# The power layer moved into the block of the layers ahead of it, its first two batches prepared inside the last gated blocks

## The chip, the cores and the metric

One core of one Trainium2 chip runs the kernel. The metric is the device time of one execution in microseconds. Engines are named by their function: TensorE (PE in the rows), VectorE (DVE), ScalarE (ACT), GpSimd (POOL) and SyncE (SP), whose queue issues most DMAs.

## The reference

Two transformer layers on x of 16 batches x 256 tokens x 128. Each half adds the layer norm of its result to x.

```python
x = x + _layernorm(_L0_attn_ref(_layernorm(x), ...))   # softmax attention, 16 heads of 8
x = x + _layernorm(_L0_ffn_ref(_layernorm(x), ...))    # softmax attention, then 8 gated experts + a shared one
x = x + _layernorm(_L1_attn_ref(_layernorm(x), W))     # "power" attention
x = x + _layernorm(_L1_ffn_ref(_layernorm(x), ...))    # routed mixture with capacity

# the power attention
qkvgr = einsum('btc,oc->bto', x, W)                    # q, k, v, and one gate per head
log_g = log_sigmoid(gates); log_G = cumsum(log_g, axis=1)
S  = einsum('bhtd,bhsd->bhts', Q, K)
Z  = 2 * log(abs(S) + 1e-7) + log(scale) + log_G[t] - log_G[s], causal mask
P  = exp(Z - rowmax);  y = (P @ V) / sum(P)
```

The kernel computes P as (|S| + eps)^2 times exp of the decays log_G[t] - log_G[s].

## The kernel before, in words

The kernel is written out instruction by instruction, each engine with its own program, and engines meet at semaphores. It has these stages, one behind the other: `load_weights`, `soft_layers` (both softmax attentions as 32 steps) and `gated_layer` share one block; then come `power_layer`, `route` and `capped_mixture`, each with semaphores and a block of its own. Where such a stage ends (`semaphores`, L190) the semaphores are cleared and all engines meet at a barrier.

The gated layer (L1806) works on 8 blocks of 512 tokens. A block has 9 experts of 2 units, so 18 units q = 0 to 17, and there are 144 units n and 72 experts x in all. For a unit TensorE makes `gate_ps` and `up_ps` (3 products of 512 columns each, `hidden`, L1953), ScalarE the Silu (`gsg`), VectorE the product (`gprod`), ScalarE its high half and GpSimd its low half (`ghid`). Two experts later TensorE makes the down product (24 products of 128 columns, `down`, L1974), and VectorE adds it up (`gacc`). `gate_ps` has two banks, `up_ps` three. Block 7 is followed by a drain step: the last halves, the down products of experts 70 and 71, three sums, the layer norm and its addition to X.

The power layer (L817) works on 16 batches b with 8 units u each (n = 8 b + u). Step t runs the scores of batch t and, in the same step, parts of other batches at the places of `POWER_AT` (L813): T (transposes of the normalized rows), QK, V and CS (cumulated log gates) stand 14, 13, 10 and 7 units ahead of a batch's first score. They use one PSUM bank in turns. So the lead-in consists of the steps -3, -2 and -1, in which only batches 0, 1 and 2 are normalized, projected and spread. Behind QK, SyncE spreads the halves of Q and K over partitions with 12 DMAs a batch; behind CS, 6 DMAs write the decay rows into M. For unit n TensorE makes the decays (L1399, L1413), near blocks (L1417) and far scores (L1431), VectorE |score| (L1292), ScalarE exp of the decays (L1144) and the square (L1134), GpSimd their product (L955), and TensorE multiplies by V (L1447).

In the lead-in, `keep_awake` (L1385, products of L1388) gives TensorE work of no use between the waits; `AGAIN` (L1398) repeats the first decay product twice in each unit of batch 0 and of batches 14 and 15.

## Time and profile before

| What | us |
|---|---|
| median of 3 timed runs | 1249.94 (1248.51 to 1253.93) |
| the profiled execution, its own time | 1247.25 |
| its span, first to last instruction | 1245.5 |
| TensorE busy | 1130.0 (91%) |
| VectorE busy | 984.0 (79%) |
| ScalarE busy | 853.6 (69%) |
| GpSimd busy | 660.0 (53%) |
| mean granted TensorE clock | 0.96 |

Times of the trace are microseconds from the start of the span. The gated layer's last products end shortly before 788, the power layer's first instruction starts at 795.05, and its units run to about 1087. A busy share is a mean over stages with different limits, so a stage is read by windows and by its own timeline. The granted clock is a share of full speed: 1.00 is 2.4 GHz, 0.50 is 1.2 GHz, and a value between them is a mean over a window with both.

### The profile page before, as it was taken

What the parts mean: (1) busy time and instruction counts of PE and PEld (TensorE: products, weight loads), DVE (VectorE), ACT (ScalarE), POOL (GpSimd) and SP (SyncE); (2) the same over time, 40 slices, a digit from 0 to 9 for tenths busy, and PEclk for the clock granted to TensorE, in tenths of its full rate; (3) what the DMA queues carried; (4) which work ended last, traced back from release to release, by engine and by line L of the source; (5) the groups of instructions that cost most, each with busy time, mean ns of one, the idle gap of its engine ahead of it and who ended that gap; (6) DMA issues with size and microseconds to landing.
All of it is one profiled execution on the core that took longest, in us unless ns stands there. A gap on an engine that the chain in (4) does not pass through costs nothing. (4 is left out here: it accounts for less than half of the span.)

```text
span 1245.5 us, 33564 instructions
## 1 busy us (share of the span) xinstructions
PE 1130.0 (91%) x11805; PEld 636.4 (51%) x11805; DVE 984.0 (79%) x2700; ACT 853.6 (69%) x1834; POOL 660.0 (53%) x688
## 2 busy tenths in 40 slices
PE   5899999999999989999999999789999999947875
PEld 2344444444444444666666666436566665524652
DVE  4899999999999995788888888449799999864223
ACT  1688888888888887655565565258799999724314
POOL 3243343454334321566565566448688888725763
PEclk9999999999999998999999999889799999956998
DMA  4111111111111110000000000013122111023117
GB/s 118 34 39 40 41 41 36 40 39 43 40 39 41 41 28 2 1 2 2 2 1 2 2 2 1 5 33 99 44 55 56 39 35 38 19 81 93 49 47 202
DMA packets 83363, 48.91 MB, mean 39 GB/s; under 512 B 17335, under 2 KB 80256, under 8 KB 83200
## 3 DMA queue, kind: packets, MB, share of 16 engines
q1 hardware_dynamic: 80720, 42.62, 13.2%
q0 software_dynamic: 1792, 3.70, 1.1%
q8 instruction: 97, 1.59, 0.5%
q14 instruction: 66, 0.54, 0.1%
q10 hardware_dynamic: 688, 0.46, 0.1%
HBM read 16.52 MB, written 10.26 MB: 22 GB/s over the span
## 5 line engine op out<-in xcount | busy, mean ns | idle before, releaser
L626 DVE TENSOR_REDUCE mxsS<-scoreS 128x2 f32<-128x512 f32 x512 | 328.8, 685 | 40.9 <-PE scoreS L765 35.6
L514 ACT ACTIVATE PTS<-stS 128x512 f32<-128x512 f32 x512 | 283.5, 591 | 55.0 <-PE stS L769 54.6
L1912 POOL TENSOR_TENSOR ghid<-gprod,ghid 128x512 f16<-128x512 f32 x144 | 165.4, 1159 | 139.1 <-ACT ghid L2041 137.3
L765 PE MATMUL scoreS<-QK 31*128 31x256 f16 x1024 | 172.5, 280 | 25.8 <-DVE mxsS L626 13.8
L955 POOL TENSOR_TENSOR PTP<-PTP,EP 128x512 f32<-128x512 f32 x128 | 162.8, 1282 | 62.1 <-ACT PTP L1134 62.0
L769 PE MATMUL stS<-QK 32*128 32x256 f16 x1024 | 168.6, 277 | 1.3 <-ACT PTS L514 1.3
L690 PE MATMUL pvS<-PTS,Vx 128*32 128x256 f32 x2048 | 139.6, 391 | 0.4
L1292 DVE TENSOR_SCALAR AP<-score_psP 128x768 int32<-128x768 int32 x128 | 121.6, 950 | 23.1 <-PE score_psP L1431 22.3
L2041 ACT ACTIVATE ghid<-gprod 128x512 f16<-128x512 f32 x144 | 90.0, 625 | 65.9 <-DVE gprod L2144 65.8
L765 PEld LDWEIGHTS scoreS<-QK 31*128 31x128 f16 x1024 | 53.8, 93 | 147.2 <-DVE mxsS L626 94.5
L2035 ACT ACTIVATE gsg<-gate_ps 128x512 f32<-128x512 f32 x144 | 84.7, 588 | 54.4 <-PE gate_ps L1965 53.9
L1134 ACT ACTIVATE PTP<-AP,epsP 128x768 f32<-128x768 f32 x128 | 119.2, 931 | 3.1 <-DVE AP L1292 2.7
L387 POOL TENSOR_TENSOR rsS<-veS,halfS 128x2 f32<-128x2 f32 (+1 forms) x32 | 28.0, 874 | 172.4 <-DVE veS L594 90.4
L1970 PE MATMUL up_ps<-ghT,split 128*128 128x512 f16 x432 | 116.8, 379 | 0.0
L1965 PE MATMUL gate_ps<-ghT,split 128*128 128x512 f16 x432 | 116.7, 379 | 0.0
L2144 DVE TENSOR_TENSOR gprod<-gsg,up_ps 128x512 f32<-128x512 f32 x144 | 95.4, 682 | 26.6 <-ACT gsg L2035 18.7
L1982 PEld LDWEIGHTS down_ps<-split,ghid 128*128 128x128 f16 x1728 | 102.4, 98 | 17.1 <-POOL ghid L1912 0.6
L1982 PE MATMUL down_ps<-split,ghid 128*128 128x128 f16 x1728 | 108.1, 219 | 0.4 <-POOL ghid L1912 0.4
L1144 ACT ACTIVATE EP<-decay_psP 128x512 f32<-128x512 f32 x128 | 75.7, 591 | 29.6 <-PE decay_psP L1413 29.2
L690 PEld LDWEIGHTS pvS<-PTS,Vx 128*32 128x32 f32 x2048 | 54.1, 110 | 49.5 <-issue 21.6
L1970 PEld LDWEIGHTS up_ps<-ghT,split 128*128 128x128 f16 x432 | 42.1, 98 | 51.2 <-DVE gprod L2144 0.7
L2156 DVE SCALAR_TENSOR_TENSOR gacc<-down_ps,gcomb,gacc 128x128 f32<-128x128 f32 x224 | 62.7, 342 | 0.5 <-PE down_ps L1982 0.5
(321 smaller groups left out, 2246.9 us busy)
## 6 DMA issues: line engine op xcount, KB each, us to landing
QK<-HLS SPq DMA_DIRECT2D x384, 32.0 KB, 1.9
QK<-HLP SPq DMA_DIRECT2D x192, 32.0 KB, 1.9
expert_outputs<-tzero SPq DMA_DIRECT2D x8, 512.0 KB
cgot<-expert_outputs SPq DMA_DIRECT2D x16, 256.0 KB, 5.0
tokens<-XB SPq DMA_DIRECT2D x16, 128.0 KB, 2.4
out_dram<-X SPq DMA_DIRECT2D x8, 256.0 KB, 2.3
wi<-L_ffn_experts_inter_dram SPq DMA_DIRECT2D x1, 1792.0 KB, 9.2
wo<-n_L_ffn_experts_out_dram SPq DMA_DIRECT2D x7, 256.0 KB, 3.2
```

Of the source, the lines that this page charges most:

```text
L514: act.activation(PT[:, n % NPT, :], st_ps[:, (NS * t + n) % 3, :], ACT.Exp, scale=SCALE).then_inc(s_exp, 1)
L626: dve.tensor_reduce(mxs[:, u // 4, :, at], score_ps[:, n % 2, :].rearrange("p (c s) -> p c s", c=TC), AX.X, ALU.max).then_inc(s_max, 1)
L690: last = pe.matmul(pv_ps[32 * j:32 * j + 32, q], Vx[:, t % 3, c, 4 * g + j, :], PT[:, (4 * g + (j ^ 2)) % NPT, S * c:S * c + S], start=(c ...
L765: scored = pe.matmul(score_ps[:, k, cols], QK[part, new, g, 0, rows], QK[part, new, g, 1, :], start=True, stop=True)
L769: turned = pe.matmul(st_ps[:, (NS * t + n) % 3, cols], QK[part, old, g, 1, rows], QK[part, old, g, 0, :], start=True, stop=True)
L955: eng.tensor_tensor(w, w, E[:, n % NE, :], ALU.mult).then_inc(s_wd if n % NU in MULT_BY_DVE else s_wp, 1)
L1134: act.activation(PT[:, n % NW, :], A[:, n % NA, :], ACT.Square, bias=eps[:, 0:1]).then_inc(s_sq, 1)
L1292: dve.tensor_scalar(A[:, n % NA, :].bitcast(I32), score_ps[:, n % 2 * WU:n % 2 * WU + WU].bitcast(I32), 0x7FFFFFFF, None, ALU.bitwise_and) ...
L1912: pool.tensor_tensor(hid[:, n // FC % NHID, 1, c, :], prod[:, n % NPROD, :], hid[:, n // FC % NHID, 0, c, :], ALU.subtract).then_inc(s_hid, 1)
L1965: last = pe.matmul(gate_ps[:, n % 2, :], gate_w[:, lw, e, cols], hT[:, n // NQ % 2, lh, :], start=(k == 0), stop=(k == 2))
L1970: last = pe.matmul(up_ps[:, n % 3, :], up_w[:, lw, e, cols], hT[:, n // NQ % 2, lh, :], start=(k == 0), stop=(k == 2))
L1982: last = pe.matmul(down_ps[:, x % 2, t * D:(t + 1) * D], hid[:, x % NHID, lh, c, t * P:(t + 1) * P], down_w[:, lw, x % EX, c, :], start=(c ...
```

## The change

`power_layer` no longer opens a block. It takes its semaphores from the common set and returns one program for each engine and four guest functions, which other stages call at named places. Tiles come from regions with fixed offsets: its buffers lie where the experts' weights and the soft layers' tiles lay; PT over the gated layer's tiles; wi and wo over the gated weights. Those writers wait for the gated layer's last readers (`gated.s_hid`, `gated.s_down`, `gated.s_acc`, `gated.s_sg`, `gated.s_prod`).

- T, QK, V and CS of batches 0 and 1 run as guests in gated blocks 6 and 7, with the moments of batches 0 to 2, the fixed rows of M and the zeros of Vk. All of them use one PSUM bank. The steps of the power layer begin at 0.
- The root of the guests' layer norm is GpSimd's `pow` instead of ScalarE's Ln and Exp. The log sigmoid of the gates of both batches is made in one go (Abs, Exp, Ln). Their `fac` is copied out raw, and its Exp comes in the power layer's first step.
- `keep_awake` is gone, and so is `AGAIN` for batch 0.
- The gated drain step is cut up: down product 70 behind the near blocks of power unit 0, down product 71 in unit 1, the sums in units 0 and 1, the moments in unit 4, the root behind unit 6, the last addition in unit 1 of step 1.
- The moments of gated block 0 stand a few units earlier in the soft layers. Regions of later stages are laid out by hand; their instructions are the same.

The diff, cut to its core:

```diff
-    STEPS = range(-3, NB + 5)
-    AWAKE, AGAIN = {("T", 0): 24, ("QK", 0): 3, ("V", 0): 5, ("CS", 0): 4, ("QK", 1): 3, ("V", 1): 5, "scores": 6}, 2
+    STEPS, AGAIN, EARLY_CS = range(NB + 5), 2, 2
+    UNITS, ADDED = 144, 72
...
+        def guest_scalar(act, what, t):
...
+            elif what == "softplus":
+                act.wait_ge(free["V"], EARLY_CS)
+                act.activation(gl[:], gx[:], ACT.Abs).then_inc(s_ge, 1)
+                act.wait_ge(s_ge, 2 * EARLY_CS + 1)
+                act.activation(gl[:], gl[:], ACT.Exp, scale=-1.0).then_inc(s_ge, 1)
+                act.wait_ge(s_ge, 2 * EARLY_CS + 2)
+                act.activation(gl[:], gl[:], ACT.Ln, bias=1.0).then_inc(s_ge, 2 * EARLY_CS - 2)
...
+                if n == 0:
+                    act.wait_ge(gated.s_hid, UNITS)
+                if n == 2:
+                    act.wait_ge(gated.s_acc, ADDED)
                 act.activation(PT[:, n % NW, :], A[:, n % NA, :], ACT.Square, bias=eps[:, 0:1]).then_inc(s_sq, 1)
...
+            elif what == "gates":
+                dve.wait_ge(s_ge, 4 * EARLY_CS)
+                reach(dve, full["CS"], t)
+                dve.scalar_tensor_tensor(lg[:], gx[:, t, :, :], 0.0, gl[:, t, :, :], ALU.min, ALU.subtract)\
+                   .then_inc(s_lg, 1)
...
+        def cumulate(pe, t):
+            pe.wait_ge(s_lg if t < EARLY_CS else free["V"], t + 1)
...
             def decays(n):
                 t, u = n // NU, n % NU
-                if n == 0:
-                    keep_awake(AWAKE["scores"])
+                if n < 2:
+                    pe.wait_ge(gated.s_sg, UNITS - 1 + n)
                 if u == 0:
                     pe.wait_ge(s_m, 96 * (t + 1))
                 reach(pe, s_taken, n - 1)
-                for _ in range(AGAIN if t >= NB - 2 or t == 0 else 0):
+                for _ in range(AGAIN if t >= NB - 2 else 0):
...
+                gated.scalar(act, {(6, 15): guest("T", 0), (6, 17): guest("QK", 0), (7, 2): guest("V", 0),
+                                   (7, 3): guest("T", 1), (7, 5): guest("QK", 1), (7, 7): guest("V", 1),
+                                   (7, 8): guest("softplus", 0), (7, 11): guest("CS", 0), (7, 14): guest("CS", 1)})
+                power.scalar(act, {(0, 0): opening})
...
+                gated.drain_vector(dve, 0)
+                power.vector(dve, {(0, 0): lambda: gated.drain_vector(dve, 1), (0, 1): lambda: gated.drain_vector(dve, 2),
+                                   (0, 4): lambda: gated.drain_vector(dve, 3), (1, 1): lambda: gated.drain_vector(dve, 4)})
...
+                gated.tensor(pe, {(6, 14): guest("T", 0), (6, 16): guest("QK", 0), (7, 1): guest("V", 0),
+                                  (7, 3): guest("T", 1), (7, 4): guest("QK", 1), (7, 6): guest("V", 1),
+                                  (7, 10): guest("CS", 0), (7, 12): guest("CS", 1)})
+                power.tensor(pe, {(-1, 7): lambda: gated.drain_tensor(pe, 0), (0, 1): lambda: gated.drain_tensor(pe, 1)})
```

TensorE before, from the last gated unit over the barrier into the lead-in. L1965 and L1970 are the gate and up products, L1982 the down products of experts 69, 70 and 71, L1388 the filler:

```order
L1965 MATMUL gate_ps<-ghT,split 128x512 x3
L1970 MATMUL up_ps<-ghT,split 128x512 x3
L1982 MATMUL down_ps<-split,ghid 128x128 x72
L2483 UNCONDITIONAL_BRANCH
L1332 UNCONDITIONAL_BRANCH
L1388 MATMUL decay_psP<-cstb 128x512 x24
L1339 MATMUL miscP<-cst,yP 128x128 x2
L1388 MATMUL decay_psP<-cstb 128x512 x3
L1345 MATMUL miscP<-yTP,wq 128x256
L1345 MATMUL miscP<-yTP,wk 128x256
L1388 MATMUL decay_psP<-cstb 128x512 x5
L1350 MATMUL miscP<-wv,yTP 128x144 x2
```

TensorE after, from the last gated unit (L2088, L2093; down products L2067) into power unit 0 (L1491 to L1525). The rows of near blocks (L1507, L1511) alternate four times; two of the four stand here:

```order
L2088 MATMUL gate_ps<-ghT,split 128x512 x3
L2093 MATMUL up_ps<-ghT,split 128x512 x3
L2067 MATMUL down_ps<-split,ghid 128x128 x24
L1491 MATMUL decay_psP<-cstb 128x512
L1507 MATMUL decay_psP<-MP 128x128
L1511 MATMUL score_psP<-QK 128x128
L1507 MATMUL decay_psP<-MP 128x128
L1511 MATMUL score_psP<-QK 128x128
```

```order
L2067 MATMUL down_ps<-split,ghid 128x128 x24
L1525 MATMUL score_psP<-QK 128x128 x2
L1491 MATMUL decay_psP<-cstb 128x512
```

Between the last gated unit and the first decay product one down product is left of three, and neither a branch nor filler; the second piece follows the first one's near blocks.

TensorE after, units 136 to 138 of block 7. L1434 to L1438 are CS of batch 0, which before stood in the lead-in:

```order
L2088 MATMUL gate_ps<-ghT,split 128x512 x3
L2093 MATMUL up_ps<-ghT,split 128x512 x3
L1434 MATMUL misc_aP<-cst,lgP 16x256
L1435 MATMUL misc_aP<-cst,lgP 16x128
L1437 MATMUL misc_aP<-lgP,cst 128x16
L1438 MATMUL misc_aP<-lgP,cst 128x16
L2088 MATMUL gate_ps<-ghT,split 128x512 x3
L2093 MATMUL up_ps<-ghT,split 128x512 x3
L2067 MATMUL down_ps<-split,ghid 128x128 x24
L2088 MATMUL gate_ps<-ghT,split 128x512 x3
L2093 MATMUL up_ps<-ghT,split 128x512 x3
```

The four products of CS stand between unit 136 and unit 137, in the midst of gated work.

ScalarE before, at the seam. L2041 is the high half of units 142 and 143:

```order
L2041 ACTIVATE ghid<-gprod 128x512 x2
L2483 UNCONDITIONAL_BRANCH
L1053 UNCONDITIONAL_BRANCH
L1136 ACT_TABLE_LOAD
L1087 ACTIVATE lvP<-mvP,epsP 128x2
L1089 ACTIVATE rsP<-lvP 128x2
```

ScalarE after, units 133 to 136 of block 7. L2154 is Silu, L2141 the high half, L1112 to L1116 are Abs, Exp and Ln of the gates:

```order
L1107 ACTIVATE Vx<-misc_aP 128x32x8
L1109 ACTIVATE gxP<-misc_aP 128x32
L2154 ACTIVATE gsg<-gate_ps 128x512
L2141 ACTIVATE ghid<-gprod 128x512
L1112 ACTIVATE glP<-gxP 128x64
L1114 ACT_TABLE_LOAD
L1114 ACTIVATE glP<-glP 128x64
L1116 ACT_TABLE_LOAD
L1116 ACTIVATE glP<-glP 128x64
L2154 ACT_TABLE_LOAD
L2154 ACTIVATE gsg<-gate_ps 128x512
L2141 ACTIVATE ghid<-gprod 128x512
```

Three table loads stand between the Silu of unit 134 and that of unit 135, where before there was none between two Silus. The load at the power layer's start stays.

## Rows read from the trace of the kernel before

**Rows 1.** Windows of whole stretches; columns: window, us, busy (x count) of five engines, clock, DMA.

```profile
680.00:720.00 40.00, 38.53 (x369) 24.93 (x368) 35.48 (x116) 23.50 (x46) 24.65 (x23) 1.00 0.01 1
786.00:795.00 9.00, 1.51 (x24) 1.34 (x24) 5.14 (x22) 0.00 (x0) 1.20 (x2) 0.89 0.00 1
795.00:820.00 25.00, 18.80 (x79) 8.92 (x79) 5.16 (x20) 6.71 (x21) 9.85 (x11) 0.90 0.08 19
875.00:890.00 15.00, 15.00 (x127) 8.76 (x130) 9.44 (x23) 10.71 (x26) 10.54 (x11) 0.50 0.13 34
```

**Rows 2.** Timeline, block 7: start us, us, engine, line, operation [idle <- releaser].

```profile
776.50 0.81 PE L1965 MATMUL gate_ps<-ghT,split 128*128 128x512 f16 x3
...
777.35 0.60 ACT L2035 ACTIVATE gsg<-gate_ps 128x512 f32<-128x512 f32 x1 [1.21 <-PE gate_ps L1965]
...
777.84 0.62 ACT L2041 ACTIVATE ghid<-gprod 128x512 f16<-128x512 f32 x1
...
778.40 0.69 DVE L2144 TENSOR_TENSOR gprod<-gsg,up_ps 128x512 f32<-128x512 f32 x1 [1.66 <-ACT gsg L2035]
...
779.09 1.50 PE L1982 MATMUL down_ps<-split,ghid 128*128 128x128 f16 x24
...
780.43 0.81 PE L1965 MATMUL gate_ps<-ghT,split 128*128 128x512 f16 x3
```

**Rows 3.** Timeline, table load of the gated layer's start, softplus and log gates.

```profile
489.71 1.28 ACT L2035 ACT_TABLE_LOAD   x1
491.00 1.14 ACT L2035 ACTIVATE gsg<-gate_ps 128x512 f32<-128x512 f32 x2
...
807.66 0.23 ACT L1078 ACTIVATE geP<-geP 128x32 f32<-128x32 f32 x1
...
807.92 0.19 DVE L1193 SCALAR_TENSOR_TENSOR lgP<-miscP,geP 128x32 f32<-128x32 f32 x1 [1.88 <-ACT geP L1078]
```

**Rows 4.** Timeline, gated tail, SyncE's decay rows, TensorE's first decay, first score.

```profile
783.02 2.84 PE L1982 MATMUL down_ps<-split,ghid 128*128 128x128 f16 x48
...
815.34 3.44 SPq L979 DMA_DIRECT2D MP<-partsP  x6
...
820.00 0.67 PE L1398 MATMUL decay_psP<-cstb 128*128 128x512 bf16 x2 [4.27 <-DMA MP<-partsP]
...
821.88 0.96 DVE L1292 TENSOR_SCALAR AP<-score_psP 128x768 int32<-128x768 int32 x1 [6.20 <-PE score_psP L1431]
```

**Rows 5.** Windows, batches 0, 1, 3, 4 and 5 of the power layer.

```profile
821.88:839.26 17.38, 16.77 (x145) 7.68 (x144) 10.48 (x20) 13.27 (x27) 10.02 (x9) 0.85 0.11 27
839.26:854.75 15.49, 15.12 (x215) 9.31 (x214) 13.16 (x26) 13.62 (x27) 12.14 (x11) 1.00 0.50 153
...
870.16:893.28 23.12, 22.43 (x215) 12.91 (x214) 16.14 (x38) 15.56 (x33) 15.28 (x15) 0.63 0.16 40
893.28:909.37 16.09, 15.99 (x221) 9.95 (x220) 15.36 (x39) 14.42 (x33) 12.16 (x12) 1.00 0.15 41
909.37:925.44 16.07, 15.97 (x221) 9.96 (x220) 15.19 (x39) 14.96 (x35) 13.96 (x14) 1.00 0.21 57
```

**Rows 6.** Timeline, TensorE's V, decay, CS, T, QK and far score.

```profile
836.02 0.76 PE L1350 MATMUL miscP<-wv,yTP 128*128 128x144 f32 x4
...
840.70 0.39 PE L1399 MATMUL decay_psP<-cstb 128*128 128x512 bf16 x1
...
841.35 0.61 PE L1356 MATMUL miscP<-cst,lgP 128*16 128x256 f32 x2
...
842.65 0.28 PE L1431 MATMUL score_psP<-QK 31*128 31x128 f16 x2
...
843.52 0.44 PE L1339 MATMUL miscP<-cst,yP 128*128 128x128 f32 x2
...
845.54 0.70 PE L1345 MATMUL miscP<-yTP,wq 128*128 128x256 f32 x2
...
846.60 0.28 PE L1431 MATMUL score_psP<-QK 31*128 31x128 f16 x2
```

More of the change, by code:

```diff
@@ L986, in store @@
                 sp.dma_start(rows[:, part, 0:D], Y[:, part, :]).then_inc(s_stored, 16)
-            sp.wait_ge(s_zero, 5)
+            sp.wait_ge(s_zero, 9)
+            for t in range(2):
+                spread(t)
+            for t in range(EARLY_CS):
+                spread_decays(t)
             for t in STEPS:
                 if t == 1:
+                    sp.wait_ge(gated.s_down, ADDED)
                     sp.dma_start(wi[:], dram["L1_ffn_experts_inter"].rearrange("e d f -> d e f")).then_inc(s_w, 16)
@@ L996, in _ @@
                     store(t - 4)
-                if has(t + 1):
+                if t >= EARLY_CS - 1 and has(t + 1):
                     spread_decays(t + 1)
@@ new lines, in power_layer, with transposes, project @@
+        ident = cst[:, C_IDENT:C_IDENT + P]
+        def transposes(pe, t):
+            pe.wait_ge(s_y, 2 * t + 2)
+            for c in range(TC):
+                last = pe.transpose(bank("T")[:, c * P:(c + 1) * P], y[:, c, :], ident)
+            last.then_inc(full["T"], 1)
+        def project(pe, t):
+            pe.wait_ge(free["T"], t + 1)
+            for k, name in enumerate(("wq", "wk")):
+                last = pe.matmul(bank("QK")[:, k * S:(k + 1) * S], w[name][:], yT[:], start=True, stop=True)
+            last.then_inc(full["QK"], 1)
@@ L1438, in times_v @@
                 reach(pe, s_os, NG * t + g)
+                if t == 0 and g == 0:
+                    pe.wait_ge(gated.s_acc, ADDED)
                 if g == 0:
@@ L1449, in times_v @@
                 last.then_inc(s_pv, 1)
+            decays(0)
+            near_blocks(0)
+            guests[-1, 7]()
             for t in STEPS:
@@ L1950, in head_tensor, with down, drain_tensor, tensor @@
                 score(pe, 0)
-        def tensor(pe):
+        def down(pe, x):
+            pe.wait_ge(s_hid, FC * (x + 1))
+            if x < 2:
+                pe.wait_ge(soft.free[("PR", "YT")[x]], SOFT_STEPS)
+            reach(pe, s_acc, x - 1)
+            for t in range(TB):
+                for c in range(FC):
+                    for k, (lh, lw) in enumerate(PARTS):
+                        last = pe.matmul(down_ps[:, x % 2, t * D:(t + 1) * D],
+                                         hid[:, x % NHID, lh, c, t * P:(t + 1) * P], down_w[:, lw, x % EX, c, :],
+                                         start=(c == 0 and k == 0), stop=(c == FC - 1 and k == 2))
+            last.then_inc(s_down, 1)
+        def drain_tensor(pe, k):
+            down(pe, EXPERTS - 2 + k)
+        def tensor(pe, guests):
             def hidden(n):
@@ new lines, in rows_and_gates @@
+                def rows_and_gates():
+                    power.guest_vector(dve, "rows", 0)
+                    power.guest_vector(dve, "gates", 1)
+                soft.vector(dve, {(-3, 5): lambda: load.vector(dve), (last - 2, 6): lambda: gated.head_vector(dve, 0),
+                                  (last - 1, 1): lambda: gated.head_vector(dve, 1),
+                                  (last, 2): lambda: gated.head_vector(dve, 2),
+                                  (last, 5): lambda: gated.head_vector(dve, 3)})
```

557 lines of the change are left out of this document (322 added, 235 removed).

## The prediction, made before the changed kernel was run

> **What bounds the kernel now.** I first read the windows: the last steady stretch of the gated layer, the seam behind it, and the lead-in of the power layer [rows 1]. In the gated layer TensorE is busy for 38.53 of 40 us at full clock, VectorE for 35.48, ScalarE for 23.50 and GpSimd for 24.65: TensorE sets the pace. From 786 to 795 TensorE works for 1.51 of 9 us, and from 795 to 820 it shows 18.80 of 25 us, nearly all of it filler that keeps its clock up. In the same 25 us the useful engines work for 5.16 (VectorE), 6.71 (ScalarE) and 9.85 us (GpSimd): nothing is full, so this stretch is a chain of waits. Then I read the power layer batch by batch [rows 5]: from batch 4 on a batch takes 16.07 to 16.09 us with TensorE busy for 15.97 to 15.99, so TensorE is the bound there too, with VectorE (15.19) and ScalarE (14.96) close behind. Batch 0 (17.38) and batch 3 (23.12) are the odd ones, and both carry a lower granted clock. Last I read the timeline for the edges: the last gate and up products (unit 143) are over at 783.02, where the down products start; and the first |score| of the power layer (L1292, my mark for "batch 0 begins") starts at 821.88 [rows 4]. That is 38.9 us from 783.02, and the change attacks them.
>
> **What goes.** The gated drain, the barrier, and the lead-in (normalize, T, QK, V, CS of batch 0 and 1, their spreads over the DMA queue) all lie one behind the other in those 38.9 us. After the change the first score needs, behind 783.02: the down product of expert 69 (half of the 2.84 us of two, 1.42), decay and near blocks of unit 0 (840.70 to 841.35, 0.65), the down product of expert 70 (1.42), the far score (0.28). That is 3.8 us, so batch 0 would begin at 786.8 if nothing had been added earlier [rows 4, 6].
>
> **What is added on TensorE.** The lead-in products of two batches now stand in TensorE's row in the gated layer, where it is the bound, so they count in full: T 0.44, QK 1.06 (845.54 to 846.60), V 0.76, CS 1.30 (841.35 to 842.65), together 3.56 us, twice, 7.1 us [rows 6]. The filler and the doubled decay products of batch 0 go and cost nothing.
>
> **What is added elsewhere.** VectorE gets about the 5.16 us of the lead-in, GpSimd its 9.85 us and three roots that ScalarE took before, spread over the last two blocks, which last some 75 us (18 pairs of units at 3.93 and what is between them). VectorE has 4.5 us of slack in 40, GpSimd 15, and VectorE has no next block's moments and routing to do in block 7 [rows 1, 2]. I price both at nothing: TensorE's rings of two gate banks and three up banks cover a partner that is late by a unit, and it idles for only 1.5 us in 40 although VectorE is busy for 35.48. If that cover is gone, the bound is the whole 5.2 us.
>
> **What is added on ScalarE, the one wait I expect.** The gated layer uses Silu, the softplus of the gates Exp and Ln. The order shows three table loads around it (before Exp, before Ln, before the next Silu). A load takes 1.28 us and the next activation starts 0.01 us behind it [rows 3]. I count from the start of the gate product of unit 134, 0. Silu starts at 0.85 (776.50 to 777.35) and takes 0.60; the high part 0.62; Abs, Exp and Ln at 0.23 each 0.69, three loads 3.84: ScalarE is back at 6.60. Silu of unit 135 takes it to 7.20, VectorE's product (0.69) to 7.89, its log gates (0.19) to 8.08. TensorE meanwhile does a pair of units with its down product in 3.93 us (776.50 to 780.43) and a unit without one in 1.30 (half of 776.50 to 779.09), so unit 136 is over at 5.23; the next in its row is CS of batch 0, which waits for these log gates. It waits 2.9 us [rows 2, 3]. While it waits, all behind it waits, the gate product of unit 137 too; that one would have waited for ScalarE until 7.20 anyway, and is no second price. For CS of batch 1 ScalarE and VectorE are ready within some 0.1 us of TensorE by the same count. Bounds: 0 (the loads hide in ScalarE's idle time, 16.5 us in 40) and 8.1.
>
> The Trainium skill, "ScalarE: Activation LUTs", section "What ACT_TABLE_LOAD costs", puts every switch at about 2.66 us, a 1283 ns load and a drain of about 1380 ns. By that rule the three switches would take 4.1 us more, the wait would be 7.0 and not 2.9 us, and the end 4 us later than my sum. The trace agrees on the load and shows no drain behind it, at 489.71 after a running ScalarE.
>
> **The DMA queue.** Decay of unit 0 waits for the rows of M that SyncE issues in 3.44 us; TensorE went on at 820.00, 1.2 us behind the last issue of 815.34 [rows 4]. In the new order rows of batch 0 are ready at some 13.3 on the count above; 3.44 and 1.2 behind is 18. TensorE comes there at 783.02 + 1.42 less 764.7 (unit 134's start, four pairs of 3.93 before 780.43), 19.7, plus 2.9 and 2.6 for the two CS: 25. So it hides; a slip of 7 us would show. The wait for the down product of expert 71 ahead of the load of wi is over a batch earlier than SyncE comes to it.
>
> **Batch 0.** It begins at 786.8 + 7.1 + 2.9 = 796.8, 25.1 us earlier than 821.88. Its length: before, 17.38 at clock 0.85 with doubled decay products. Now TensorE has 11.1 us of work there (8 units of 0.65 + 0.28, one each of T, QK and V, one down product), ScalarE the 13.27 us of before and 0.6 for the last high part. Queued behind the waits: TensorE's down product 71 (1.42) waits for ScalarE's high part and GpSimd's low part of unit 143; VectorE's sum of it stands in front of |score| of unit 2; ScalarE's square of unit 2 waits for that sum. Behind the first far score TensorE has 0.65 + 0.28 + 0.65 + 1.42 = 3.0 us up to the end of down product 71; the sum is four VectorE instructions, 0.9 us at the tail's mean of 0.23 (22 in 5.14 us, rows 1). So unit 2 comes 3.9 us behind unit 0, where two units of a steady batch take 4.0. I take 15.5, as batch 1 has (15.49); bounds 13.9 (ScalarE's work alone) and 23.1 (a whole batch at the lower clock) [rows 5]. Gain 1.9 us.
>
> **The sum.** 25.1 + 1.9 = 27.0 us off the profiled execution's own 1247.25 (span 1245.5 and 1.75 around it): 1220.3. That execution is 2.7 us below the median of the timed runs (1249.94) and 1.3 below the fastest. Taken off the median it is 1222.9. I say 1222. The gated drain now lies beside batch 0 and 1, everything from batch 4 on is as it was.
>
> **The rivals.**
> A. As above, with one stretch at the lower clock as before: 1222, own range 1218 to 1227.
> B. The fall in batch 3 goes. There the granted clock is 0.50 (1.2 of 2.4 GHz) from 875 to 890 although TensorE shows 15.00 of 15 us busy, and the batch takes 23.12, not 16.09: 7.0 us. In the whole batch TensorE waited for only 0.7 us (22.43 busy) [rows 1, 5]. Batches 4 to 13 do the same work at 1.00. If the new start shifts this away: 1215. For it: it happens once in 14 like batches. Against it: it may belong to the order of work in batch 3, which is unchanged.
> C. The clock falls in batch 0. Without the doubled decays TensorE is busy for 11 of 15.5 us there, less than in any full batch of before, and no filler stands ahead. In batch 0 ScalarE hides the slower products, but the level held for some 17 us in batch 3, so half a batch or a whole one behind it pays up to 7.6 us (23.12 less 15.49): 1226 to 1230. The Trainium skill, "TensorE: Matmul & The Clock Gate", section "What's actually happening", says the default state is throttled and activity releases it. By that rule the seam's fall goes with the idle stretch, which is in A already; whether batch 0 has activity enough no row here shows.
> D. The table loads cost what the bound says (8.1 us and not 2.9), or VectorE's added work does: 1227.
> E. Slower than before. The clock falls at batch 0 and does not come back while batches are TensorE bound. Each batch at half costs 7.0 us, so the gain of 27.0 is gone after four batches, and from the fifth on it is over 0.5% slower: five batches give 1222 + 35 = 1257. For it: it held through a full TensorE once. Against it: it came back by itself after 17 us, and after the far longer idle of the seam within batch 0.
> That the change doesn't do what it says (batch 0 still waits for the gated end) would show as units 0 to 2 stretched by the last high and low part; by the order it is at most 3 us.
>
> **Chances.** A 0.54, B 0.16, C 0.18, D 0.08, E 0.04. From 1212 to 1232 holds all of A, nearly all of B, C and D. A measurement of this kernel tells a change from none from about 0.5% (6.2 us) on; all but E and accidents of the same size lie beyond it: faster 0.94, same 0.02, slower 0.04.
>
> **What would show it.** In the profile after: no gap over 2 us on TensorE between the last gated unit and the first score, and no filler; the |score| of unit 0 at about 797, that of batch 1 at 812; a wait of about 3 us on TensorE for VectorE's log gates in the middle of block 7, with three table loads on ScalarE ahead of it; no wait of the first decay product for a DMA; units 0 to 2 of batch 0 within 4 to 5 us; batches 1 and 2 at 15.5. The prediction is wrong if the gated blocks 6 and 7 grow by more than 12 us, if the first decay waits for M, or if the granted clock is at the lower level for more than one batch.

## The result, and the profile after

The changed kernel takes 1233.84 us (median of 18 runs, 1229.66 to 1246.35) against 1249.8 for the kernel before, run beside it (18 runs); ratio 0.9872, 95% interval 0.9849 to 0.9895. It is faster by 16 us. Forecast were 1222 and the range 1212 to 1232: the direction came out, the size did not, and of the 28 us that were to go 16 went. The profiled execution took 1234.57 us (span 1232.7), where the sum had given 1220.3: 14.3 us more.

First the windows of batch 0 to 3 in the profile after (us, then the busy time of each engine, the granted clock, the share of the DMA engines), each batch from its first |score| to the next one's:

```profile
800.63:818.64 18.01, 15.59 (x147) 8.42 (x146) 13.05 (x35) 12.59 (x23) 12.12 (x11) 0.72 0.05 14
818.64:840.37 21.73, 19.44 (x215) 11.63 (x214) 16.43 (x31) 13.93 (x28) 11.78 (x10) 0.76 0.35 110
840.37:855.78 15.41, 15.23 (x215) 9.30 (x214) 14.28 (x33) 13.96 (x29) 12.59 (x12) 1.00 0.13 35
855.78:872.37 16.59, 15.35 (x215) 9.30 (x214) 15.87 (x39) 14.13 (x32) 13.50 (x14) 1.00 0.17 47
```

Against [rows 5]: batch 0 and 1 are longer (17.38 and 15.49 before) and carry the lower clock. Batch 3 takes 16.59 and not 23.12, its clock is 1.00. Batch 0 begins at 800.63 where 796.8 was forecast.

The same view of two blocks of the gated layer, each from its first gate product to the next block's: block 5, which has no guests, and block 6, which has them.

```profile
671.59:709.38 37.79, 36.32 (x343) 23.18 (x341) 33.27 (x108) 22.20 (x44) 22.60 (x20) 1.00 0.01 1
709.38:752.02 42.64, 39.19 (x349) 25.37 (x347) 38.43 (x119) 22.79 (x46) 31.33 (x34) 0.96 0.01 2
```

Block 6 of the kernel before took 37.45 us, so the block is 5.2 us longer. T and QK of batch 0 explain 1.1 us of it: from the first start of each to the start of the product behind it are 0.22 and 0.86 us. Against block 5 VectorE is busy for 5.2 us more and GpSimd for 8.7. The timeline of that block, TensorE first, says where TensorE stops (the bracket is the idle time before, and what ended it; down products in between are left out):

```profile
733.40 0.81 PE L2088 MATMUL gate_ps<-ghT,split 128*128 128x512 f16 x3
736.19 0.82 PE L2093 MATMUL up_ps<-ghT,split 128*128 128x512 f16 x3 [1.98 <-DVE gprod L2298]
738.49 0.46 PE L2047 MATMUL gturn_ps<-router,ghT 128*128 128x8 f16 x12 [1.47 <-DVE ghT L2192]
...
740.72 2.53 PE L2067 MATMUL down_ps<-split,ghid 128*128 128x128 f16 x24
```

VectorE in the same place. `gve` is the variance, the input of the norm's root:

```profile
727.64 0.98 DVE L2274 TENSOR_SCALAR gve<-gmv 128x4 f32<-128x4 f32 x1
...
732.14 2.67 DVE L2280 TENSOR_SCALAR gtmp<-gacc,gmv,grs 128x128 f32<-128x128 f32 x4 [1.30 <-POOL grs L2006]
734.85 0.69 DVE L2283 TENSOR_TENSOR X<-X,gtmp 128x512 f32<-128x512 f32 x1
735.46 1.28 DVE L2298 TENSOR_TENSOR gprod<-gsg,up_ps 128x512 f32<-128x512 f32 x2
```

And GpSimd ahead of it. `yP` is a guest, `ghid` the gated layer's own low part, `grs` the root:

```profile
726.66 0.80 POOL L1040 TENSOR_SCALAR yP<-X,mvP,rsP 128x128 f32<-128x128 f32 x1
727.43 1.16 POOL L2011 TENSOR_TENSOR ghid<-gprod,ghid 128x512 f16<-128x512 f32 x1
728.58 0.79 POOL L1040 TENSOR_SCALAR yP<-X,mvP,rsP 128x128 f32<-128x128 f32 x1
729.95 1.16 POOL L2011 TENSOR_TENSOR ghid<-gprod,ghid 128x512 f16<-128x512 f32 x1 [0.58 <-ACT ghid L2141]
731.07 1.04 POOL L2006 TENSOR_TENSOR grs<-gve,ghalf 128x4 f32<-128x4 f32 x1
732.07 1.17 POOL L2011 TENSOR_TENSOR ghid<-gprod,ghid 128x512 f16<-128x512 f32 x1
733.17 1.05 POOL L1030 CAST MP<-cst 128x1024 bf16<-128x1024 f32 x1
```

The block's own norm on VectorE waits for a root that GpSimd gives at 732.1, 22.7 us behind the start of the block, where block 5 has it at 21.3. The way to that delay goes over VectorE. The guest at 726.66 pushes the low part to 727.43; the variance starts 0.21 us behind it and ends with it, after 0.98 us in place of the 0.17 of block 5. The product, ScalarE's high part, the next low part and the root behind it are late in turn. Ahead of that low part GpSimd is idle for 0.58 us, so the guest at 728.58 costs the root nothing. Then the four subtractions take 2.67 us beside GpSimd's low part and cast, where in block 5 they took 1.94; the product is late, and TensorE waits 1.98 us for it, a wait that block 5 does not have. The 1.47 us of wait a little later stand in block 5 too and are no child of the change. After that the down product of two halves takes 2.53 us and not 1.50: the clock has gone to its lower level.

In the middle of block 7 stands the wait that was forecast. ScalarE:

```profile
772.59 1.28 ACT L1114 ACT_TABLE_LOAD   x1
773.89 0.26 ACT L1114 ACTIVATE glP<-glP 128x64 f32<-128x64 f32 x1
774.22 1.28 ACT L1116 ACT_TABLE_LOAD   x1
775.51 0.26 ACT L1116 ACTIVATE glP<-glP 128x64 f32<-128x64 f32 x1
775.79 1.28 ACT L2154 ACT_TABLE_LOAD   x1
777.08 0.60 ACT L2154 ACTIVATE gsg<-gate_ps 128x512 f32<-128x512 f32 x1
```

VectorE, GpSimd and TensorE behind it:

```profile
777.71 0.69 DVE L2298 TENSOR_TENSOR gprod<-gsg,up_ps 128x512 f32<-128x512 f32 x1 [1.18 <-ACT gsg L2154]
778.27 2.27 POOL L2011 TENSOR_TENSOR ghid<-gprod,ghid 128x512 f16<-128x512 f32 x2 [3.62 <-ACT ghid L2141]
778.31 1.16 DVE L1269 SCALAR_TENSOR_TENSOR lgP<-gxP,glP 128x32 f32<-128x32 f32 x1
779.62 0.59 PE L1434 MATMUL misc_aP<-cst,lgP 128*16 128x256 f32 x2 [4.36 <-DVE lgP L1269]
...
781.23 1.44 PE L2088 MATMUL gate_ps<-ghT,split 128*128 128x512 f16 x3
```

Three loads, as counted, no drain behind any. The wait is 4.36 us and not 2.9: ScalarE comes 0.6 us later than my count, and the log gates take 1.16 us in place of the 0.19 of [rows 3]. They begin 0.04 us behind the first of two low parts of GpSimd (2.27 us for both) and end when it ends. The gate product behind the wait takes 1.44 us and not 0.81.

Last, batch 1. The windows, with the granted clock in the last column but two:

```profile
808.00:818.00 10.00, 9.20 (x75) 4.59 (x73) 5.63 (x15) 6.71 (x13) 7.87 (x8) 0.50 0.07 19
818.00:824.00 6.00, 5.95 (x97) 3.50 (x91) 5.39 (x10) 4.99 (x9) 3.83 (x3) 1.00 0.27 58
824.00:826.00 2.00, 0.21 (x8) 0.09 (x2) 1.97 (x5) 0.11 (x1) 0.00 (x0) 1.00 0.89 302
826.00:829.00 3.00, 2.50 (x18) 1.25 (x18) 2.91 (x10) 2.48 (x6) 2.03 (x2) 0.86 0.99 372
829.00:839.00 10.00, 10.00 (x94) 6.16 (x93) 5.43 (x10) 6.00 (x12) 5.92 (x6) 0.53 0.11 29
```

And the timeline around 824:

```profile
821.53 2.74 DVE L2280 TENSOR_SCALAR gtmp<-gacc,gmv,grs 128x128 f32<-128x128 f32 x4
824.30 0.69 DVE L2283 TENSOR_TENSOR X<-X,gtmp 128x512 f32<-128x512 f32 x1
824.91 0.95 DVE L1369 TENSOR_SCALAR AP<-score_psP 128x768 int32<-128x768 int32 x1
...
825.92 0.28 PE L1525 MATMUL score_psP<-QK 31*128 31x128 f16 x2 [1.79 <-DVE AP L1369]
```

The last norm of the gated layer stands as one piece of 3.4 us between the |score| of unit 1 and that of unit 2. The score tile has room for two units, so TensorE runs out and stands still: it works for 0.21 of 2 us. The piece is that long because its first two subtractions take 0.90 and 1.41 us and end within 0.1 us of GpSimd's products beside them; the other two take 0.33 and 0.34. The four subtractions of block 7, from 774.69 on, take 1.11 us with GpSimd idle. From 829 to 839 TensorE shows 10.00 of 10 us busy at a clock of 0.53. At the same time the load of wi runs (DMA share 0.89 to 0.99), which makes it a suspect of its own.

Where the 14.3 us are, profile against forecast (what the forecast left alone is taken from the profile before): work ahead of the gated layer's first gate product −1.8; from there to batch 0 +5.7 (the stretch lost 19.4 us, 332.92 to 313.49, and not 25.1); batch 0 +2.5 (18.01, not 15.5); batch 1 +6.2 (21.73, not 15.49); batch 3 −6.5; the other batches, the end of the power layer and the routing −1.6; the mixture of experts at the end +9.8 (109.0 to 118.8). The three items around the seam, +5.7, +2.5 and +6.2, make 14.4; the others nearly cancel.

### The profile page after: what moved, and what is told of

Same layout as the page of the kernel before. It is cut to its first block and busy times, and to the rows that moved or that the text cites. A ratio compares the mean times of both kernels' runs of the same rounds, so it can differ in the third digit from the quotient of the medians.

```text
span 1232.7 us, 33441 instructions
## 1 busy us (share of the span) xinstructions
PE 1114.3 (90%) x11739; PEld 632.8 (51%) x11739; DVE 991.0 (80%) x2703; ACT 854.8 (69%) x1831; POOL 662.2 (54%) x695
## 5 line engine op out<-in xcount | busy, mean ns | idle before, releaser
L2141 ACT ACTIVATE ghid<-gprod 128x512 f16<-128x512 f32 x144 | 90.0, 625 | 66.5 <-DVE gprod L2298 66.4
L2154 ACT ACTIVATE gsg<-gate_ps 128x512 f32<-128x512 f32 x144 | 84.7, 589 | 60.3 <-PE gate_ps L2088 60.0
L2093 PE MATMUL up_ps<-ghT,split 128*128 128x512 f16 x432 | 118.1, 383 | 2.0 <-DVE gprod L2298 2.0
L2088 PE MATMUL gate_ps<-ghT,split 128*128 128x512 f16 x432 | 117.4, 381 | 0.0
L2067 PEld LDWEIGHTS down_ps<-split,ghid 128*128 128x128 f16 x1728 | 103.5, 99 | 17.4 <-issue 0.8
L2067 PE MATMUL down_ps<-split,ghid 128*128 128x128 f16 x1728 | 109.3, 220 | 0.0
L2093 PEld LDWEIGHTS up_ps<-ghT,split 128*128 128x128 f16 x432 | 42.4, 98 | 53.9 <-DVE gprod L2298 2.8
```

Of the source, the lines that this page charges most:

```text
L2067: last = pe.matmul(down_ps[:, x % 2, t * D:(t + 1) * D], hid[:, x % NHID, lh, c, t * P:(t + 1) * P], down_w[:, lw, x % EX, c, :], start=(c ...
L2088: last = pe.matmul(gate_ps[:, n % 2, :], gate_w[:, lw, e, cols], hT[:, n // NQ % 2, lh, :], start=(k == 0), stop=(k == 2))
L2093: last = pe.matmul(up_ps[:, n % 3, :], up_w[:, lw, e, cols], hT[:, n // NQ % 2, lh, :], start=(k == 0), stop=(k == 2))
```

## The experiments

**Both kernels once more** (before_2, after_2), to see what belongs to chance.

> The kernel before again, unchanged. Theory 1 (falls of the clock come by chance): batch 3 takes 16 and not 23 us or another batch takes 22 to 23, and the mixture's stage has another length than 109 us. Rival (they belong to the kernel): batch 3 takes 23 us again and the mixture 109.

> The changed kernel again, unchanged. In its first profile the stage of the routed mixture (from its first gather to the last instruction) took 119 us, in the one of the kernel before 109. Theory 1 (the granted clock falls in this stage by chance, whatever the kernel): another profile gives another length, anywhere from 108 to 120. Rival (the new places of its tiles, or what the power layer leaves behind, slow it): 119 again, within 1 us. Batch 0 begins at 800 to 801, batch 1 takes 21 to 22 us again if that fall is the kernel's own.

Measured: before 1242.7, after 1231.43. Before's batch 3 now takes 16.60 at clock 1.00. After's batches 0 and 1 repeat: 18.22 and 21.40, clocks 0.72 and 0.76, and so does the stretch ahead of batch 0. The mixture takes 110.5 and 112.1. Between these two the stretch from the first gate product to batch 0 lost 17.4 us (331.28 to 313.90), where the first two profiles had lost 19.4: the kernel before is the one that varies. So the long batches 0 and 1 belong to the change; the fall in batch 3 and the +9.8 in the mixture do not. Over all 13 profiles of this study, kernels of either kind, the fall in batch 3 is whole in three (before, again0, split), in part in one (noload: 19.0) and absent in nine; the mixture is at 109 to 112 in twelve, and at 118.8 in the one execution above. In that one TensorE waits twice for 3.8 us for gathered rows, where after_2 has 1.0 and 2.6; why they came late was not tried.

**Doubled decay products in batch 0 again** (again0).

```
-  for _ in range(AGAIN if t >= NB - 2 else 0):
+  for _ in range(AGAIN if t >= NB - 2 or t == 0 else 0):
```

> Changed kernel with the doubled first decay products (two more of 512 columns a unit) back in batch 0. Theory 1 (TensorE is too lightly loaded in batch 0, its clock falls and batch 1 pays): the granted clock stays at 1.00 through batches 0 and 1, batch 1 takes 15.5 and not 21.7 us, batch 0 about 16 to 17, whole kernel 6 to 8 us faster than the changed one. Rival (the clock falls for something behind batch 0, such as the waits on the gated drain): batch 1 stays at 21 to 22 us, batch 0 gets 1 to 2 us longer, the total within 2 us of the changed kernel.

Measured: 1230.24 us (6 runs), ratio to before 0.9878 [0.9837, 0.9919], no different from the changed kernel's. In the profile batch 0 has clock 1.00 and takes 16.28 us, batch 1 still 18.49 at 0.91. With the doubled products the clock of batch 0 stays up, worth 1.7 us there. Batch 1 keeps a standstill (1.35 us) and a low clock behind it, 3.4 us long in place of 10.2, so neither expectation fits: it is 3.2 us shorter and not back at 15.5. In this profile batch 3 has its fall (23.15).

**Softplus without its table loads** (noload; Exp and Ln replaced by Copy: the gates' softplus is left out).

```
-  act.activation(gl[:], gl[:], ACT.Exp, scale=-1.0)
+  act.activation(gl[:], gl[:], ACT.Copy)
-  act.activation(gl[:], gl[:], ACT.Ln, bias=1.0)
+  act.activation(gl[:], gl[:], ACT.Copy)
```

> Changed kernel with Copy in place of the two activations Exp and Ln of the gates' softplus (that part of the result is left out), so no table load stands between two Silus. Theory 1 (the wait of 4.4 us before CS of batch 0 and the lower clock behind it are the table loads): the wait is under 0.5 us, the clock stays at 1.00 up to the first score, batch 0 begins 5 to 6 us earlier, about 795; the total 5 to 6 us less. Rival (TensorE's guests wait for VectorE or GpSimd, which the guests have filled): the wait stays at 2 us or more and batch 0 begins at 798 to 800.

Measured: 1227.93 us (8 runs), ratio 0.9858 [0.982, 0.9897]. Units 134 to 143 take 22.63 us in place of 25.72, with this wait:

```profile
785.42 0.59 PE L1434 MATMUL misc_aP<-cst,lgP 128*16 128x256 f32 x2 [2.94 <-DVE lgP L1269]
```

Without any load 2.94 of 4.36 us are left, so the rival holds for the wait. What goes is 1.42 us, and 0.98 of that is the log gates, which take 0.18 us here with no low part beside them. What is left is VectorE: its log gates stand behind a product and the norm of block 6, whose root GpSimd gives at 781.87 and whose first subtraction takes 1.17 us beside a low part. The theory holds for the clock, which stays at 1.00 through block 7. Batch 0 begins 3.1 us earlier, counted from the first gate product. Then the clock falls inside batch 0, at 811.4, and stays low until 838.7, almost to the end of batch 1 (21.96 us).

**CS one pair of units later, one table set for Exp and Ln** (late). VectorE's rows and log gates of CS move by the same two units.

```
+  act.preload_act_table_set("natural_log_exp_and_others")
-  (7, 8): guest("softplus", 0), (7, 11): guest("CS", 0), (7, 14): guest("CS", 1)    # ScalarE
+  (7, 8): guest("softplus", 0), (7, 13): guest("CS", 0), (7, 15): guest("CS", 1)
-  (7, 10): guest("CS", 0), (7, 12): guest("CS", 1)                                  # TensorE
+  (7, 12): guest("CS", 0), (7, 14): guest("CS", 1)
```

> The changed kernel with the two CS guests (and the high parts, rows and log gates that go with them) one pair of units later in block 7, and with one ScalarE table set that serves Exp and Ln loaded ahead of them, so two table loads stand there in place of three. Theory (the wait of 4.4 us ahead of CS is ScalarE's and VectorE's lateness behind the loads, and the lower clock behind it is its child): the wait falls to under 1.5 us, no granted clock under 1 in block 7, and units 134 to 143 take 21 to 23 us in place of 25.7; batch 0 begins 3 to 4.5 us earlier. Rival (TensorE is held there by VectorE's norm of block 6 as well, so that only the share of the loads goes): units 134 to 143 take 24 us, batch 0 begins under 2 us earlier. The time by the theory is 1230, by the rival 1232.

Measured: 1228.18 us (6 runs), ratio 0.9857 [0.9819, 0.9896]. Units 134 to 143 take 21.18 us; no wait ahead of CS is left, one of 1.37 us stands ahead of a gate product for the silu behind the loads. Block 6 and the eight units behind it together take 61.1 us here and in pair, which has the changed kernel's own gated layer, and 60.5 in the changed kernel: up to there the edit changes nothing. Batch 0 begins 3.9 us earlier, counted from the first gate product. The theory holds. But batch 1 now is as bad as it gets:

```profile
798.08:815.37 17.29, 14.02 (x147) 7.94 (x146) 14.01 (x35) 12.26 (x23) 12.16 (x11) 0.82 0.05 14
815.37:840.95 25.58, 25.58 (x215) 14.25 (x214) 15.08 (x32) 14.36 (x28) 12.14 (x10) 0.52 0.30 94
```

TensorE is busy for all of 25.58 us: 10 us more than a batch needs, and no standstill. The clock had fallen ahead of the batch, at 809.3 inside batch 0, as TensorE came out of a wait of 1.33 us for a |score|, and it rose only at 840.0:

```profile
809.30:815.37 6.07, 5.97 (x53) 3.35 (x53) 4.14 (x8) 3.55 (x8) 4.60 (x5) 0.50 0.14 37
815.37:840.00 24.63, 24.63 (x208) 13.62 (x207) 14.48 (x30) 13.55 (x26) 12.14 (x10) 0.50 0.30 96
```

In the changed kernel the fall of batch 0 (807.7 to 817.9) is over before batch 1 begins, and a second one follows the standstill (828.2 to 838.4). So a batch 1 that is too long has two forms.

**The last norm in five pieces** (split). Its four subtractions and the addition at unit 7 of batch 0, units 0, 1 and 4 of batch 1 and unit 1 of batch 2.

```
-  (1, 1): lambda: gated.drain_vector(dve, 4)
+  (0, 7): lambda: gated.drain_vector(dve, 4), (1, 0): lambda: gated.drain_vector(dve, 5),
+  (1, 1): lambda: gated.drain_vector(dve, 6), (1, 4): lambda: gated.drain_vector(dve, 7),
+  (2, 1): lambda: gated.drain_vector(dve, 8)
```

> The changed kernel with the last norm of the gated layer (four tensor_scalar and one add, 3.43 us in one piece on VectorE at unit 1 of batch 1) cut into five pieces at five places, from unit 7 of batch 0 to unit 1 of batch 2. Theory (TensorE's gap of 2.06 us at 824 in batch 1 is the |score| of that unit, held behind this piece, and the fall of the clock from 829 on is its child): no wait of TensorE over 0.8 us in batch 1, granted clock 1.00 there from 829 on, batch 1 at 16 to 17 us in place of 21.7. Rival 1 (the gap is the child of the 1.8 MB load of wi that runs at the same time): gap and fall stay, batch 1 at 21 to 22. Rival 2 (the clock falls in batch 1 whatever stands there, as it fell in batch 0): gap gone, clock still 0.7 to 0.8, batch 1 at 19 to 21. Whole time by the theory 1229, by the rivals 1232 to 1234.

Measured: 1232.2 us (6 runs), ratio 0.9879 [0.9841, 0.9918]; in the profile batch 3 takes 23.18. The windows of batch 0 and 1:

```profile
801.72:820.07 18.35, 15.85 (x153) 8.56 (x154) 13.30 (x36) 12.93 (x24) 12.14 (x11) 0.72 0.05 14
820.07:835.66 15.59, 14.90 (x214) 9.15 (x210) 14.87 (x29) 13.57 (x27) 11.89 (x10) 1.00 0.46 143
```

Batch 1 is at 15.59 with clock 1.00 although batch 0 in front of it has 0.72, and with the load of wi in it (DMA share 0.46 of the batch). TensorE has no wait over 0.4 us in it. So in the form that the changed kernel shows, the norm in one piece causes both the standstill and the low clock behind it; both rivals fall. The whole time is nevertheless the one expected by the rivals. The fall in batch 3 can account for that: four of the six runs have the mean granted clock of the profiled one (0.952 to 0.954) and 1231.4 to 1235.3 us, the other two 0.960 and 1225.6 and 1228.3. Only one of the six was profiled.

**The fixed rows out of block 6** (thin). Seven pieces of GpSimd work that depend on nothing.

```
-  (6, 0): guest("fixed", 0), (6, 1): guest("fixed", 1), (6, 4): guest("fixed", 2), ... (6, 14): guest("fixed", 6)
+  (1, 0): guest("fixed", 0), (1, 13): guest("fixed", 1), (2, 13): guest("fixed", 2), ... (5, 15): guest("fixed", 6)
```

> The changed kernel with the seven pieces of fixed rows (casts into M, zeros into Vk, about 6 us of GpSimd) taken out of block 6 and put one by one into blocks 1 to 5. Theory (block 6 is 5.2 us longer because GpSimd, which takes 31.3 of 42.6 us there in place of 22.6 of 37.5, answers late and holds VectorE's instructions, so that TensorE waits for products): block 6 takes 39 to 40.5 us in place of 42.6, blocks 1 to 5 grow by under 0.3 us each, batch 0 begins 2 to 3.5 us earlier. Rival (VectorE's own added work, T, QK and moments guests, is what makes it longer): block 6 stays within 0.5 us of 42.6. Time by the theory 1231, by the rival 1234.

Measured: 1229.2 us (6 runs), ratio 0.985 [0.981, 0.9889]. Block 6 takes 41.08 us, 1.5 less; no earlier block grows by over 0.05. Alone that says little, since block 6 takes 41.5 to 43.2 us in the seven profiles that have the changed kernel's own guests in it. What is short there comes back in the next eight units (units 126 to 133 of the 144), so both are taken together from here on: 60.1 to 61.1 us in those seven, 58.9 here. So 1.2 to 2.2 us go, less than the theory asked for: the casts are a part of it.

**The two normalizing guests behind the root** (norms).

```
-  (6, 6): guest("norm0", 0), (6, 7): guest("norm1", 0),
+  (6, 8): guest("norm0", 0), (6, 9): guest("norm1", 0),     # the root of the block's norm is at (6, 8), ahead of guests
```

> The changed kernel with only the two normalizing guests of GpSimd in block 6 moved behind the root of the block's own norm (and the casts and zeros behind them one unit on). Theory (the root that VectorE's norm waits for stands behind two pieces of 0.8 us each, so it comes late): the norm's first tensor_scalar begins 21.0 to 21.3 us behind the start of block 6 as in block 5, in place of 22.7, and block 6 takes 41 to 41.5 us in place of 42.6. Rival (the root is late because the silus and products ahead of it are late, whatever GpSimd does in between): block 6 within 0.3 us of 42.6.

Measured in one execution: 1228.67 us. Block 6 takes 39.75 us, 2.9 less:

```profile
730.08 1.01 POOL L2006 TENSOR_TENSOR grs<-gve,ghalf 128x4 f32<-128x4 f32 x1
731.08 0.80 POOL L1040 TENSOR_SCALAR yP<-X,mvP,rsP 128x128 f32<-128x128 f32 x1
```

The block begins at 709.16 here, so the root begins 20.9 us behind it (21.7 in the changed kernel). The low part ahead of VectorE's variance now starts 0.8 us earlier and is in its last 0.15 us when the variance starts, which takes 0.18 us in place of 0.98; all behind it comes that much earlier. TensorE's wait at this place is 0.73 and not 1.98 us. Two pieces of work were moved by two units, and of three behind them two by one unit and one by two. Of the 2.9 us 1.3 come back in the next eight units and 0.7 behind them: with those eight units it is 58.9 us against 60.1 to 61.1, as much as in thin, by one profile each. Batch 1 has the second form: the clock falls at 810.8, inside batch 0, and rises at 841.6; batch 1 takes 25.59 us.

**The two edits behind the gated layer alone** (pair: the doubled products and the five pieces, as above).

> The changed kernel with only two edits, both behind the gated layer: doubled decay products in batch 0, and the last norm in five pieces. Theory (what lies behind the start of batch 0 costs 8 to 9 us more than forecast, by these two causes alone, and what lies ahead of it 5 to 6 by causes of its own): batch 0 still begins at 801 to 804, batch 0 takes 16.3 us, batch 1 15.2 to 15.6, both at clock 1.00; time 1225 to 1226 where batch 3 runs at full clock. Rival (the late start in block 7 and the lower clock there carry on into batch 0): batch 1 stays at 17 or over.

Measured: 1220.06 us (6 runs, 1216.33 to 1224.07), ratio 0.9805 [0.9774, 0.9836], against the changed kernel's 0.9872 [0.9849, 0.9895].

```profile
804.07:820.71 16.64, 15.03 (x169) 7.80 (x167) 13.81 (x36) 13.00 (x24) 12.09 (x11) 1.00 0.04 11
820.71:836.05 15.34, 14.86 (x212) 9.08 (x206) 14.48 (x30) 13.45 (x27) 11.76 (x10) 1.00 0.47 149
```

Batches 0 and 1 take 31.98 us in place of 39.74, 7.8 us less, while what lies ahead of batch 0 is as in the changed kernel (314.5 and 313.5 us from the first gate product). Batch 2, with the last of the five pieces, takes 16.00 and not 15.41. The 7.8 us less these 0.6 are half of the miss of 14.4. The whole time came out 5 us under the expected one.

**All of it at once** (best1), with the guests of block 6 in both new orders (fixed rows out, norm guests behind the root, here at units 9 and 11).

> All of it at once: CS guests later with the common table set, last norm in five pieces, fixed rows out of block 6 and the two normalizing guests of block 6 behind the root of the block's own norm, doubled decay products in batch 0. If the costs are separate and each theory holds: block 6 at 39 to 40, units 134 to 143 at 22, batch 0 begins at 793, batch 0 at 16 us, batch 1 at 16, together 13 us off the changed kernel's stretch up to batch 2; with a fall of the clock of 7 us in batch 3, which comes and goes from chip to chip, 1221 to 1228. If they are one cost that only moves (VectorE and GpSimd are simply full): under 5 us off, 1229 or more.

Measured: 1213.51 us (6 runs, 1212.77 to 1216.33), ratio 0.9744 [0.971, 0.9779]: the costs are separate. In ratio the forecast of 1222 was 0.9777. In the profile block 6 and the next eight units take 57.7 us, 3.1 less than in the mean of the seven, units 134 to 143 21.16, the stretch up to batch 0 306.6 (6.9 less than in the changed kernel), and batch 0 and 1 together 7.9 less:

```profile
797.63:814.27 16.64, 15.03 (x169) 7.80 (x168) 13.81 (x35) 13.00 (x24) 12.11 (x11) 1.00 0.04 11
814.27:829.50 15.23, 14.82 (x212) 9.07 (x206) 14.44 (x30) 13.47 (x27) 11.78 (x10) 1.00 0.47 150
```

The expectation puts the fall in batch 3 down to the chip. It does not follow the chip: seven profiles, from late to cool, come from one chip, and only split's shows it.

**The same without the doubled products** (cool).

> The version with everything at once, but with the decay products of batch 0 not doubled. Theory (TensorE's share of idle time in batch 0 brings its clock down, and the level then lies on the batch behind it, whatever that batch does; no idle stretch elsewhere is needed for it): granted clock 0.7 to 0.85 in batch 0, batch 0 at 17.3 to 18.3 us in place of 16.64, batch 1 at 18 to 25 in place of 15.23, so the time is 4 to 11 us longer than 1213.5. Rival (the doubled products only cost TensorE's time; the lower clock came from the gaps in block 7 and in batch 1, which this version does not have either): clock 1.00 in both batches, batch 0 at 15.5 to 16.3, the time 1212 to 1213.

Measured: 1212.38 us (6 runs, 1209.22 to 1224.58), ratio 0.977 [0.9727, 0.9814].

```profile
792.56:809.75 17.19, 13.52 (x153) 7.88 (x154) 14.26 (x36) 12.93 (x24) 12.14 (x11) 0.90 0.05 13
809.75:825.08 15.33, 14.90 (x214) 9.15 (x210) 14.58 (x30) 13.56 (x27) 11.78 (x10) 1.00 0.46 147
```

My theory here falls: the clock does drop in batch 0, to a mean of 0.90, but batch 1 pays nothing. The rival is wrong on batch 0 (clock 0.90, 17.19 us) and right on batch 1 and the time. Over the study batch 1 takes 15.2 to 15.6 us in all four kernels that have the norm in pieces, whatever batch 0's clock (0.72, 0.90, 1.00, 1.00), and 18.5 to 25.6 in all seven executions that have it in one. In four of the seven (after, after_2, again0, thin) a standstill of 1.35 to 1.79 us stands in batch 1 and the low clock behind it. In the other three (noload, late, norms) the clock fell in batch 0 and stayed low for 27 to 31 us with no standstill in batch 1; whether the norm has a part in how long it stays low was not tried on these three alone, and that this kernel had its clock back after 3.4 us is one execution. From the start of the last gate product to batch 2 this kernel takes 37.6 us and best1 37.3, and the whole times of the two cannot be told apart: once the norm is cut, no worth of the doubled products is shown. The clock fell in batch 0 in all eight profiles without them and in none of the three of again0, pair and best1.

## Why the prediction was wrong, step by step

**What goes, and 3.8 us behind the last gated unit.** Right. The last gate product starts at 795.59 and the first |score| at 800.63, 5.04 us behind it, where the sum had 1.3 and 3.8. No filler, no barrier, no stretch of chains is left.

**What is added on TensorE, 7.1 us.** Some 1.5 us too high. The rows were read from the first start to the modelled end, but the next product starts earlier: in the gated blocks T takes 0.22, QK 0.86, V 0.49 to 0.55 and CS 1.22 us from its start to the next product's, 5.6 us for two batches at full clock. Units 126 to 133, which hold V of batch 0 and T, QK and V of batch 1, grew by 2.1 us where the sum had 3.0.

**What is added elsewhere, priced at nothing.** This is the step that failed, in two places. Ahead of batch 0 the text said that VectorE and GpSimd have slack (4.5 and 15 us in 40) and that TensorE's rings cover a partner that is late by a unit. The slack was there as a mean, but the guests stood around the one place of the block where VectorE waits for GpSimd anyway: the root of the norm, for which it idles 1.27 us in block 5 too. Cost: 4.1 us in block 6 beyond T and QK (42.64 against 37.45 + 1.1). With the eight units behind it counted in, norms and thin each take back some 1.8 us and both together 3.1. The bound named for lost cover, 5.2 us, would have held it; the value taken was at the wrong end.

A rule of the Trainium skill speaks of part of this and I had not weighed it. "SBUF — State Buffer", section "Who interferes with whom": VectorE and GpSimd share a pair of ports as an exclusive lock. A VectorE instruction in a two-port mode and a GpSimd instruction, or a VectorE instruction with two SBUF inputs and a GpSimd instruction that reads SBUF, do not run side by side: the one issued first keeps the ports and the other blocks until it is done. By that rule the log gates, whose two inputs now both lie in SBUF, would wait out the low part, and they do: 1.16 us and not 0.19. The variance in block 6 (0.98 and not 0.17) and the subtractions of the last norm (0.90 and 1.41 and not 0.33) agree too.

**The one wait I expect, 2.9 us.** The place, the releaser and the three loads were right, the size was not: 4.36 us, 1.0 of the difference the held log gates and the rest ScalarE's own lateness. The loads were not what it hung on alone: without them 2.94 us are left, VectorE's part (noload). The counting did leave out what a wait does to the products behind it: CS took 1.6 us (779.62 to 781.23) and not 1.3, the gate product 1.44 and not 0.81. Units 134 to 143 came out at 25.72, where 17.01 before, 2.6 for the two CS and 2.9 make 22.5. By the Trainium skill's rule quoted in the prediction, with a drain behind each load, the wait would have been 7.0. The trace agrees on the load, 1.28 us, and shows no drain: behind each of the three the next activation follows within 0.02 us.

**The DMA queue.** Right: no decay product waits for M.

**Batch 0, 15.5 us.** Too low by 2.5. Units 0 to 2 take 4.39 us, within the 4 to 5 forecast. At full clock the batch takes 16.3 to 16.6 (again0, pair, best1), so my estimate is 1.4 to 1.7 us for the lower clock and 0.8 to 1.1 for the rest, the drain inside it and, in those three, the doubled products. That is rival C's mechanism in its first half. Its second half, a batch behind it that pays, did not happen in the changed kernel, whose clock was back at 817.9, before batch 1; batch 1's +6.2 has another reason there. In noload, late and norms it did: 27 to 31 us at the lower level from batch 0 on, and a batch 1 of 22.0 to 25.6.

**"The gated drain now lies beside batch 0 and 1"** stood in the sum at nothing. It is the largest single miss, 6.2 us. A batch of 8 units takes some 16 us, so for each unit VectorE owes TensorE a |score| of 0.96 us within two units, some 4 us; a piece of 3.4 us between two of them breaks that, whatever VectorE's mean load is (it showed 16.43 of 21.73 us busy). The standstill is 1.79 us of wait in the changed kernel, and the low level behind it lasts 10.2 us. Where it lasts 3.4 us (again0, thin) batch 1 is 3 us too long. Cut in five, the norm leaves 15.2 to 15.6.

**The signs.** The prediction called itself wrong if gated blocks 6 and 7 grew by more than 12 us. From the first gate product of block 6 to the last of block 7 they grew by 16.0 us (70.19 to 86.21), where its own terms make 10.0.

**Rival B** was right that the fall in batch 3 may go and wrong in tying it to the new start: it comes and goes for both kernels. In the profile it hid 6.5 us of the miss, by luck, and the long mixture added 9.8, as much by luck. **Rival D** named the loads or VectorE's added work, at 5 us. The loads are 1.4 us of the wait at most; VectorE's added work, held by GpSimd, is the larger part of the 5.7 us ahead of batch 0, so D's second half held. **E** did not come: the level came back every time.

Open: why the gathered rows of the mixture came late in one execution, why the low clock held for 10 us behind the standstill in the changed kernel and for 3.4 in again0 and thin, and why a fall inside batch 0 lasted 3.4 us in cool, 10 in the changed kernel and 27 to 31 in noload, late and norms.

## What to carry to other kernels

When work is moved into a loop whose bound engine is fed by others, slack as a share of busy time does not price it: ask for each helper how long it may be away at that place, and cut what is longer than that into pieces. Ask also what a guest pushes, and onto what: here a GpSimd guest of 0.8 us moved a low part onto a VectorE instruction of 0.17 us, and a root that the chain waits for came 0.8 us late. And price a wait on TensorE with the products behind it at the lower clock: here a standstill of 1.4 to 1.8 us made its batch 3 to 6 us longer, most of it by the clock.

## What the runs showed of the hardware that I had not expected

TensorE's granted clock stayed at 0.50 to 0.53 (1.2 of 2.4 GHz) with TensorE shown busy throughout: 10.00 of 10 us in the changed kernel's batch 1, 25.58 of 25.58 us in late. In these cases it came back while the power layer's batches went on as before.

VectorE instructions of 0.17 to 0.19 us took 0.71 to 1.25 us when they began beside a GpSimd operation of 1.16 us, and ended within 0.05 us of its end: 0.71 in thin, where 0.47 us of it had passed; 0.98 where 0.21 had; 1.23 at 769.95, 0.03 us ahead of the start shown for it. With one table set that serves both Exp and Ln, loaded by name, two loads of 1.28 us did the work of three.
